# A residual chain of modulated 1-D convolutions on one Trainium2 core: the order of a sample's twelve filter products

## The reference

```python
def _layer(x, style, w, b, mw, mb, typ):
    s = style @ mw.T + mb
    weight = SCALE * w * s[:, None, :, None]
    demod = lax.rsqrt(jnp.sum(weight * weight, axis=(2, 3)) + EPS)
    weight = weight * demod[:, :, None, None]
    if typ == 'same':         # 3 taps, stride 1
        out = jax.vmap(_conv_same)(x, weight) + b[None, :, None]
    elif typ == 'upsample':   # stride 2 transposed, then blur
        ...
    elif typ == 'downsample': # blur, then stride 2
        ...
x = x + block0(x); x = x + block1(x); x = x + block2(x); x = x + block3(x)
# block: 'same', 'upsample', 'same', 'downsample'
```

## Time and profile before

| what | value |
|---|---|
| median of 3 runs | 1319.05 us (1318.85 to 1319.1) |
| span of the profiled execution, first to last instruction | 1316.0 us |
| TensorE busy | 1294.8 us, 98% of the span, 6565 products |
| VectorE busy | 1155.7 us, 88% |
| ScalarE busy | 840.8 us, 64% |
| GpSimd busy | 353.5 us, 27% |
| mean granted TensorE clock | 0.994 |

### The profile page before, as it was taken

One profiled execution on the slowest core, in us unless ns is written; L12 is line 12 of the kernel. 1 busy time (PEld: TensorE's weight loads), 2 busy tenths in 40 slices (PEclk: granted clock), 3 DMA queues, 4 the chain that ended last, 5 costly groups with the idle time before them and its releaser, 6 DMA issues.

```text
span 1316.0 us, 20135 instructions
## 1 busy us (share of the span) xinstructions
PE 1294.8 (98%) x6565; PEld 1077.2 (82%) x6565; DVE 1155.7 (88%) x1855; ACT 840.8 (64%) x1528; POOL 353.5 (27%) x632
## 2 busy tenths in 40 slices
PE   7799999999999999999999999999999999999998
PEld 6588888888888888888888888888888888888887
DVE  6898988998989899989889899989888888888885
ACT  5666566666565666666666576666566777777774
POOL 3215212133133121124131321121522253332211
PEclk8899999999999999999999999999999999999999
DMA  9235645446654465554556445565554367665643
GB/s 316 79 96 158 186 143 154 141 144 188 173 151 116 140 183 173 148 172 120 160 179 173 142 122 159 158 181 162 167 139 127 104 150 173 181 181 148 174 123 97
DMA packets 95368, 203.38 MB, mean 155 GB/s; under 512 B 10720, under 2 KB 12256, under 8 KB 95264
## 3 DMA queue, kind: packets, MB, share of 16 engines
q1 hardware_dynamic: 94896, 201.81, 53.4%
q10 hardware_dynamic: 368, 0.28, 0.1%
HBM read 72.39 MB, written 67.24 MB: 106 GB/s over the span
## 4 chain that ended last, share of the span: by engine, by line
PE 95%; DVE 3%; issue 1%; ACT 1%; POOL 0%; DMA 0%; SPq 0%; ACTq 0%; DVEq 0%; POOLq 0%
PE ps L463 93%; PE ps L565 1%; PE ps L395 1%; DVE gf L1035 0%; PE ps L443 0%; DVE gl L1071 0%; DMA gh<-gh 0%; DVE xl L978 0%; DVE vf L1014 0%; DVE vl L1021 0%; DVE gf L1041 0%; DVE vh L1023 0%; DVE zl L984 0%; ACT kp L750 0%; DVE X L993 0%
## 5 line engine op out<-in xcount | busy, mean ns | idle before, releaser
L463 PE MATMUL ps<-zh,gh 128*128 128x512 f32 (+1 forms) x1028 | 408.6, 397 | 5.8 <-DMA gh<-gh 3.7
L463 PE MATMUL ps<-zl,gh 128*128 128x512 f32 (+1 forms) x1028 | 406.4, 395 | 0.0
L721 ACT ACTIVATE zh<-ps,t_bx 128x512 fp32r<-128x512 f32 x256 | 175.5, 685 | 295.7 <-PE ps L463 293.3
L750 ACT ACTIVATE kp<-ps,t_T1s 64x256 f32<-64x256 f32 x512 | 213.2, 464 | 136.2 <-PE ps L463 132.9
L463 PE MATMUL ps<-zh,gl 128*128 128x512 f32 (+1 forms) x1028 | 282.5, 396 | 0.0
L993 DVE SCALAR_TENSOR_TENSOR X<-ps,t_D,X 128x512 f32<-128x512 f32 x255 | 189.8, 744 | 69.9 <-PE ps L463 43.8
L463 PEld LDWEIGHTS ps<-zh,gh 128*128 128x128 f32 x1028 | 194.6, 189 | 53.4 <-issue 5.2
L984 DVE SCALAR_TENSOR_TENSOR zl<-ps,t_bx,zh 128x512 fp32r<-128x512 f32 x256 | 190.5, 744 | 49.3 <-ACT zh L721 45.6
L463 PEld LDWEIGHTS ps<-zl,gh 128*128 128x128 f32 x1028 | 195.0, 190 | 45.2
L463 PEld LDWEIGHTS ps<-zh,gl 128*128 128x128 f32 x1028 | 194.1, 189 | 45.1
L978 DVE SCALAR_TENSOR_TENSOR xl<-X,t_S,xh 128x513 fp32r<-128x513 f32 x256 | 204.4, 818 | 4.5 <-ACT xh L709 2.4
(11 more groups left out here) (204 smaller groups left out, 1546.0 us busy)
## 6 DMA issues: line engine op xcount, KB each, us to landing
out_x<-X SPq DMA_DIRECT2D x255, 256.5 KB, 5.0
X<-out_x SPq DMA_DIRECT2D x96, 513.0 KB, 6.9
gh<-gh SPq DMA_DIRECT2D x127, 240.0 KB, 3.0
gl<-gl SPq DMA_DIRECT2D x127, 240.0 KB, 3.6
X<-x_in SPq DMA_DIRECT2D x32, 513.0 KB, 8.3
pk<-taps_in SPq DMA_DIRECT2D x3, 512.0 KB, 11.9
pk<-pack_in SPq DMA_DIRECT2D x3, 352.0 KB, 11.1
pk<-sets_in SPq DMA_DIRECT2D x4, 256.0 KB, 8.4
```

Of the source, the lines that this page charges most:

```text
L463: return pe.matmul(out_ap, a, b, start=first, stop=last, skip_group_check=True)
L721: act.activation(zh[n % 2][:, ZPAD:ZPAD + M], ps[:, ZP + n % 2, :], IDENT, bias=tab["bx"][:, k, b:b + 1]).then_inc(s["zhi"], 1)
L750: return act.activation(kp[rows, to, i, :], got[of, :, j, :], ACT.Copy, scale=tab["T1s"][of, k, b:b + 1])
```

## The change

In `convg`, for all samples but the last, the four products gh·zh come first, then the four gh·zl, then the four gl·zh as before. The first product waits for zhi where it waited for zlo, and the wait for zlo stands ahead of the fifth product, which is the first that reads zl. Nothing else is touched: the same 12 products, the same sums, the same tiles.

```diff
-                pe.wait_ge(s["zlo"], n + 1)
+                pe.wait_ge(s["zhi"], n + 1)
                 if n < 2:
                     pe.wait_ge(s[("gh0", "gh1")[n]], 2)
                 elif i == 0 or n == 2:
...
                 for j, c in taps_at:
                     add(o, h[:, j:j + 2, :], zh[b][:, c], first=(j == 0))
+                pe.wait_ge(s["zlo"], n + 1)
+                for j, c in taps_at:
                     add(o, h[:, j:j + 2, :], zl[b][:, c])
```

## The result

The changed kernel takes 1321.01 us (median of 11 runs, 1319.96 to 1322.14), the kernel before 1318.72 us (11 runs, 1317.03 to 1319.1). The ratio is 1.0018, with a 95% interval of 1.001 to 1.0026: slower by 2.3 us, about 0.18%. The forecast was 1318.7 us with a range from 1317.1 to 1320.6. The time lies above the range.

What follows compares the result with a forecast made beforehand. TensorE was taken to bound the kernel, through its stalls and its products' distance. Span 1316.0 - 0.85 (waits gone) + 0.5 (order) = 1315.7 us; with 3.05 us from span to median, 1318.7 us, range 1317.1 to 1320.6.

Steps and rivals of the forecast that it cites:

- What bounds the kernel: Whole kernel: TensorE busy 98% of the span and 95% of the chain; only its stalls or its products' distance pay.
- The gain at samples 52, 116 and 180: Head of convg: late starts waiting for zl go, 0.61 + 0.12 + 0.12 = 0.85 us gained.
- two covers, 0.2 and 0.93 us: Moved wait at the fifth product: 0.2 us worked out at sample 52, its tightest place; 0.93 us named among the signs.
- The added wait: Fifth product of 255 samples: satisfied when reached, taken as nothing, upper end 0.005 us each, 1.3 us; as rival, chance 12%.
- What the change moves: Reordered gh products: three zh to zh steps 0.6 ns slower in 252 samples, 0.5 us more; ends 1.1 us either way.
- the eights' 233.6 ns: Step within runs of eight gh products, zh and zl in turn; put at 232.4 ns without the delays counted.
- the fours' 233.0 ns: Step within runs of four gl products, zh in a row with new weights each time; taken for the new order.
- The fixed 396 ns: One product's time, subtracted from each run of eight or four before dividing the rest into seven or three steps.
- the 20 samples that the text counted as delayed for other reasons: From 65 us on, second filter product late behind small products: about 0.1 us each, 2 us in all, 1.2 ns a step.
- The sign of being wrong: Profile after: gh steps over 1.5 ns from 233.6 (2.6 us), or a named wait ahead of a zl product.
- The rival on shared weights: Four zl products of 252 samples: same-tap pairs cheaper by up to 5 ns a step, 5.0 us, so 1323.2 us; chance 7%.
- The chances: Whole run time: 86% within 0.2% (forecast 74%, added wait 12%), 7% faster, 7% slower.

Runs made afterwards that it cites:

- The moved wait alone: Kernel before, old order, with zhi awaited at the head of convg and zlo ahead of the second product: 1318.8 us, ratio 0.9997.
- 384 added waits: Kernel before, old order, with an already satisfied wait for zlo ahead of products two to nine of each sample: 1320.16 us, ratio 1.0011.
- the five layouts: Old and new order each as given, z tiles lengthened, z and x tiles lengthened, 32 bytes ahead of zh, 32 behind zl: ratios 0.9971 to 1.0018.
- The two padded pairs: Both orders with z tiles of 2112 bytes: old 1318.97, new 1317.26 us; with x tiles of 2112 bytes too: old 1318.65, new 1317.35 us.
- the kernel with the opposite taps: Changed kernel with the four zl products in reversed order of taps, so the fourth and fifth product share weights: 1322.37 us, ratio 1.0029.

## Why the prediction was wrong, step by step

- **What bounds the kernel: right.** TensorE is 97% of the chain that ended last, and the only thing that counted besides waits was the distance of its products. That was said, and then looked for in the wrong products.
- **The gain at samples 52, 116 and 180: right.** With the two products ahead at 303.78, an unstalled start would be 304.25; it came at 304.28, 0.03 us late instead of 0.61, and the fifth product at 305.29 for the forecast 305.24. The named waits for zl are gone. (The prediction gives this wait two covers, 0.2 and 0.93 us; the first is the one worked out from the rows.) The moved wait alone costs nothing and shows its gain in the trace.
- **The added wait: right.** Nothing was taken; 384 added waits in 48 samples cost less than a hundredth. The upper end of 0.005 us each, 1.3 us in the sum, was not used.
- **What the change moves: this step failed.** The text priced only steps between the reordered products, by the eights' 233.6 ns and the fours' 233.0 ns as properties of a pattern that go with it to another place. The products that the diff doesn't touch were put at nothing, without a reason. The sum was +0.5 us, with ends of 1.1 us either way. The runs showed that untouched products change their pace with the order: by the starts of 48 samples the twelve products lost 0.04 us, and `conv0`, K, V and the step into `conv0` lost 0.7, in all 16 ns a sample or 4.0 us for 252. Order and the places of tiles decide together, since the same change of order gives from -0.09 to +0.82 us in the five layouts.
- **The reading behind it was wrong in size as well.** The fixed 396 ns hid that the fours were slower: by starts, groups 7 to 64 of before have fours of 234.1 ns, and eights of 234.0 that are about 232.8 without the late second products. Of the 20 samples that the text counted as delayed for other reasons, three were those that waited for zl.
- **The sign of being wrong looked at the wrong place.** By the prediction's own division the gh steps of after are 234.6 ns, inside the 232 to 235 that it asked for and 1.0 ns from 233.6, where 1.5 was the alarm, and no wait was named. Its checks on the steps passed while the span, at 1318.2 us, left its 1315 to 1317.
- **The rival on shared weights ended on the right side and for another reason.** It forecast 1323.2 us if repeated weights were cheaper. The two padded pairs, in which the same loss of repeated weights costs nothing or brings a little, and the kernel with the opposite taps, in which one repeated load comes back and the time rises, speak against it. The Trainium skill (TensorE: Matmul & The Clock Gate, "Step-by-step: what each phase is for") keeps loading and computing apart so that weights are loaded once for many products. If the repeated loads of this kernel were cheaper for that reason, the old order should win in every layout. It wins in three of five, and in two of these three not within the twelve products that share or don't share their weights, but outside them.
- **The chances.** 7% for slower was too low because the one mechanism with a sign was weighed, and not the plain fact that 4600 products of 512 columns lie on the path, so that half a nanosecond on each is 2.3 us. The range should have allowed for a nanosecond of pace on all of them, 4.6 us, in both directions.

What stays open: by which rule order and places decide. It is not the place within 64 bytes alone (64 bytes more give another time), not the z tiles alone (two thirds of the 32 bytes' gain come from the tiles behind them), and not the order alone. The products of K follow the same order from the same places in the kernels before and after and yet differ by 16 ns a group, so more counts than a product, its neighbour and their places: what ran further ahead of it, or what goes on beside it. The kernel before shows this within one run: samples 124 and 136 have the same twelve products from the same tiles, and the last of the eleven steps takes 241 ns in the first (which begins at 663.51 us) and 230 in the second (724.90), ahead of which stands a sample with small products. VectorE, ScalarE and the DMAs, whose engines are busy for 0.54 of the time from 65 to 1290 us, work beside TensorE; whether they have a part in it was not tried. That the pace repeats to a hundredth from run to run and from chip to chip speaks against anything that comes at random times, but that is an argument and no test.

## What to carry to other kernels

In a kernel whose TensorE stands still nowhere, count the products on the path and multiply by one nanosecond before anything is forecast. That is the width by which an order or an unused tile moved this one (from 240.48 to 242.06 us for 864 products of 512 columns and what lies between them), and a gain below it is only worth taking together with a look at the layout. Sum the steps of the products that the change doesn't touch as well as of those that it does. Take steps from starts, not from busy time. Compare such kernels not by run times alone but by the start of one product and of the same product many rounds later, which here repeats to 0.01 us in 241. A moved or added wait that was satisfied when it was reached cost nothing that could be measured here; a new order of products did, and should be timed in two or three layouts before it is kept or dropped.

## What the runs showed of the hardware that was not expected

- The stream of products repeats from run to run to a hundredth of a microsecond in 241 us (241.28, 241.29, 241.29 in three kernels with the old order; 242.04 in four with the new). The changed kernel run again and the one with zl at zero ran on different chips and agree.
- Unused bytes in front of tiles change the pace by up to 0.66% (240.48 us with 32 bytes, 242.06 with 64, for 48 samples), and K products, with the same operands and order, take from 96.78 (old order, 32 bytes behind zl) to 100.14 us (the changed kernel) in 61 groups.
- A new order of products changes the pace of products that it doesn't touch: 0.7 of the 0.76 us lie there.
- Zeros in four of the twelve filter products change the 242.04 us of 48 samples by less than a hundredth.
- A matmul's weight load doesn't pass a wait for its moving operand: the loads of gh at sample 52 stood until zl was there, though gh was ready (after the change the same loads start at 304.25, ahead of zl). The second product after such a wait comes late too, 0.33 us behind the first instead of 0.23, so that each of the three real waits cost some 0.10 us beyond itself.
